# A transformer-like gate network on one core: the powers of the norms in two halves, and a new order of the steps in the middle batches

## The reference

```python
xn = layernorm(x)
s = attn(xn)                  # 16 heads of 16; rotary; the heads' logits are mixed (Wpre),
                              # softmax over all 512 keys, mixed again (Wpost), times v, Wout
g = silu(ffn(xn))             # 2 layers
x = x + s * g

# one layer of ffn: 8 heads of 64, windows of 128 tokens that see the window before
q, k, v = split(shift_token(x) @ wqkv)
q = l2norm(q) * q_scale;  k = l2norm(k) * k_scale      # t / max(norm(t), 1e-12)
q, k = rotary_xpos(q, k)
x = x + local_attention(q, k, v) @ wo
h = layernorm(shift_token(x)) * g + b
a, gate = split(h @ w1 + b1)
x = x + (a * gelu(gate)) @ w2 + b2
```

## Time and profile before

| | us |
|---|---|
| median of three runs | 5117.18 (5115.65 to 5125.04) |
| the profiled execution | 5116.08 |
| its span, first to last instruction | 5114.3 |
| busy: TensorE | 4966.4 |
| busy: VectorE | 3407.3 |
| busy: ScalarE | 3108.0 |
| busy: GpSimd | 2889.0 |

### The profile page before, as it was taken

The page is one execution under the profiler, slowest core; times in us unless marked ns, Lnnn a source line. Parts: engine busy times, 40 slices in busy tenths (PEclk is TensorE's granted clock), DMA queues, the critical chain, the costliest instruction groups (busy, mean ns, idle before and its releaser), DMA issues. The chain is left out here.

```text
span 5114.3 us, 184542 instructions
## 1 busy us (share of the span) xinstructions
PE 4966.4 (97%) x76184; PEld 4074.9 (80%) x76184; DVE 3407.3 (67%) x8316; ACT 3108.0 (61%) x8073; POOL 2889.0 (56%) x2509
## 2 busy tenths in 40 slices
PE   7999999999999999999999999999999999999998
PEld 5887888878878878787787877878888888878887
DVE  7667676666766667666676666766667676676765
ACT  4556665566655666556666566665566655666655
POOL 5546565565655656555565555655546555465654
PEclk9999999999999999999999999999999999999999
DMA  2321111121111211112111211211112112121111
GB/s 85 120 73 64 70 55 74 46 74 58 55 74 46 75 58 55 74 56 73 50 58 70 74 55 50 77 52 74 55 62 70 46 74 76 40 70 69 52 62 30
DMA packets 61263, 325.85 MB, mean 64 GB/s; under 512 B 6416, under 2 KB 23824, under 8 KB 43536
## 3 DMA queue, kind: packets, MB, share of 16 engines
q1 hardware_dynamic: 49632, 297.26, 15.4%
q0 software_dynamic: 10800, 16.78, 1.7%
HBM read 288.33 MB, written 34.08 MB: 63 GB/s over the span
## 5 line engine op out<-in xcount | busy, mean ns | idle before, releaser
L1603 POOL TENSOR_TENSOR q_lo<-q_mix,q_hi 128x512 fp32r<-128x512 f32 x512 | 661.0, 1291 | 868.5 <-ACT q_hi L1059 868.4
L1072 ACT ACTIVATE probs<-bank_S,neg_max 128x512 f32<-128x512 f32 x1024 | 699.2, 684 | 738.9 <-DVE neg_max L1333 645.3
L772 PE MATMUL bank_S<-k_hi,q_lo 128*128 128x512 f32 x2048 | 878.4, 429 | 38.9 <-POOL q_lo L1603 25.0
L1333 DVE TENSOR_REDUCE neg_max<-bank_S 128x1 f32<-128x512 f32 x1024 | 696.2, 687 | 301.4 <-PE bank_S L774 296.1
L773 PE MATMUL bank_S<-k_lo,q_hi 128*128 128x512 f32 x2048 | 805.0, 393 | 0.7 <-issue 0.7
L774 PE MATMUL bank_S<-k_hi,q_hi 128*128 128x512 f32 x2048 | 805.3, 393 | 0.0
L1598 POOL TENSOR_TENSOR q_mix<-q_rope,w_pre 128x256 f32<-128x256 f32 x1024 | 634.7, 647 | 43.8 <-POOL q_lo L1603 0.4
L789 PEld LDWEIGHTS bank_M<-mixer_n,probs 64*64 64x64 f32 x32768 | 529.8, 135 | 156.5 <-issue 138.0
L789 PE MATMUL bank_M<-mixer_n,probs 64*64 64x64 f32 x32768 | 597.0, 221 | 8.7 <-DVE o_locT_lo L1442 3.4
L1629 POOL TENSOR_TENSOR l_probs<-l_probs,l_inv 128x1024 f32<-128x1024 f32 (+1 forms) x256 | 430.6, 1690 | 270.5 <-DVE l_inv L1436 269.6
L1614 POOL TENSOR_TENSOR inv_norms<-norms_c,minus_half 128x16 f32<-128x16 f32 x128 | 417.1, 3258 | 259.9 <-DVE norms_c L1370 258.1
(11 more groups left out here) (160 smaller groups left out, 11374.9 us busy)
## 6 DMA issues: line engine op xcount, KB each, us to landing
w_qkv_hi<-split_qkv SPq DMA_DIRECT2D x30, 1536.0 KB, 9.6
w_qkv_lo<-split_qkv SPq DMA_DIRECT2D x30, 1536.0 KB, 6.3
w_hi<-split SPq DMA_DIRECT2D x30, 1408.0 KB, 6.1
w_lo<-split SPq DMA_DIRECT2D x30, 1408.0 KB, 6.0
w_hi<-split SPq DMA_DIRECT2D x30, 768.0 KB, 5.3
w_lo<-split SPq DMA_DIRECT2D x30, 768.0 KB, 7.2
w_o_hi<-split_o SPq DMA_DIRECT2D x30, 512.0 KB, 3.7
w_o_lo<-split_o SPq DMA_DIRECT2D x30, 512.0 KB, 4.6
```

Source lines behind the costliest of these rows:

```text
L772: mm(bank[k][:], q_lo[q], k_hi[:, s, :], start=(s == 0), stop=False)
L1072: fn(probs[:, n % PB, :], bank[k][:], ACT.Exp, bias=neg_max[:, n % 2:n % 2 + 1], accum_out=row_sum[:, n % 4:n % 4 + 1]).then_inc(emptied[k ...
L1333: v.tensor_reduce(neg_max[:, n % 2:n % 2 + 1], bank[k][:], AX.X, ALU.max, negate=True)\
L1603: g.tensor_tensor(q_lo[:, c % QB], q_mix[:], q_hi[:, c % QB].bitcast(F32), ALU.subtract)\
```

## The change

Two things. GpSimd's part of `qkv` computes k's eight powers alone and signals them with a semaphore of their own (k_inv_done). Its part of `join` waits for those and for the addition, multiplies k, and then computes q's eight powers; the wait for the last reader of the old q powers moves there with them. And ORDER, the list of a middle batch, is a new arrangement of the same 363 steps. FIRST_ORDER and LAST_ORDER are as they were.

```diff
@@ GpSimd, qkv and join
                 pool.wait_ge(clip_done, now.at(clip_done, w + 1))
                 if now.past(w):
                     pool.wait_ge(k_ready, now.at(k_ready, w))
-                if now.past(l):
-                    unit = ("local_scores", (l - 1) % LAYERS, QUADS * t + QUADS - 1)
-                    pool.wait_ge(emptied["F1"], now.fill(unit, "F1", ago=not l))
-                g.tensor_tensor(inv_norms[:, t, :], norms_c[:], minus_half[:], ALU.pow).then_inc(inv_norm_done, 1)
+                g.tensor_tensor(inv_norms[:, t, H:2 * H], norms_c[:, H:2 * H], minus_half[:, H:2 * H], ALU.pow).then_inc(k_inv_done, 1)
 
             def join(step, l, t):
                 w = TW * l + t
-                pool.wait_ge(inv_norm_done, now.at(inv_norm_done, w + 1))
+                pool.wait_ge(k_inv_done, now.at(k_inv_done, w + 1))
                 pool.wait_ge(rot_added, now.at(rot_added, w + 1))
                 k_tok = qk_tok[:, 1, :].rearrange("p (h d) -> p h d", h=H)
                 g.tensor_tensor(k_tok, k_tok, inv_norms[:, t, H:2 * H, None].to_broadcast([P, H, HD]), ALU.mult)\
                     .then_inc(k_ready, 1)
+                if now.past(l):
+                    unit = ("local_scores", (l - 1) % LAYERS, QUADS * t + QUADS - 1)
+                    pool.wait_ge(emptied["F1"], now.fill(unit, "F1", ago=not l))
+                g.tensor_tensor(inv_norms[:, t, 0:H], norms_c[:, 0:H], minus_half[:, 0:H], ALU.pow).then_inc(inv_norm_done, 1)
```

The stretches of ORDER that the prediction speaks of (the line before and after; the list in between is new as well):

```diff
@@ ORDER, the start
-expand.0 part.0 expand.1 qkv.0.0 join.0.0 part.1 scores.0 scores.1 qkv.0.1 scores.2 expand.2 bound q_turn.0.0 mixers.0
-join.0.1 part.2 k_turn.0.0 expand.3 qkv.0.2 q_turn.0.1 k_turn.0.1 scores.3 scores.4 part.3 mix.0 join.0.2 mixers.1
-expand.4 qkv.0.3 part.4 q_turn.0.2 mix.1 scores.5 join.0.3 mixers.2 k_turn.0.2 scores.6 scores.7 expand.5 mix.2
-sigmoid.0 part.5 expand.6 q_turn.0.3 k_turn.0.3 mixers.3 scores.8 part.6 local_scores.0.0 scores.9 mix.3
-local_scores.0.1 weigh.0.0 scores.10 expand.7 mixers.4 values.0 sigmoid.1 part.7 local_scores.0.2 scores.11 p_turn.0.0
-weigh.0.1 mix.4 weigh.0.2 mixers.5 scores.12 sigmoid.2 expand.8 local_values.0.0 part.8 p_turn.0.1 expand.9 scores.13
-silu mix.5 sigmoid.3 gated p_turn.0.2 local_values.0.1 mixers.6 part.9 local_scores.0.3 scores.14 scores.15
+expand.0 part.0 expand.1 qkv.0.0 part.1 join.0.0 expand.2 scores.0 scores.1 qkv.0.1 q_turn.0.0 bound join.0.1 mixers.0
+k_turn.0.0 part.2 qkv.0.2 expand.3 mix.0 scores.2 scores.3 q_turn.0.1 join.0.2 mixers.1 k_turn.0.1 part.3 expand.4
+qkv.0.3 part.4 q_turn.0.2 mix.1 scores.4 scores.5 join.0.3 k_turn.0.2 q_turn.0.3 mixers.2 sigmoid.0 expand.5 scores.6
+part.5 k_turn.0.3 scores.7 expand.6 local_scores.0.0 mix.2 mixers.3 scores.8 weigh.0.0 local_scores.0.1 part.6
+scores.9 mix.3 weigh.0.1 p_turn.0.0 scores.10 sigmoid.1 sigmoid.2 expand.7 values.0 local_values.0.0 part.7 mixers.4
+local_scores.0.2 p_turn.0.1 scores.11 expand.8 mix.4 scores.12 mixers.5 weigh.0.2 sigmoid.3 silu local_values.0.1
+gated part.8 scores.13 local_scores.0.3 expand.9 mix.5 mixers.6 p_turn.0.2 scores.14 scores.15 local_scores.0.4 part.9
@@ ORDER, end of layer 0
-out_proj.0.2 expand.13 local_values.0.6 p_turn.0.7 scores.22 local_values.0.7 mixers.10 scores.23 out_proj.0.3 mix.10
-half_turn.0 mixers.11 part.13 scores.24 expand.14 shift_turn.0 mix.11 scores.25 scores.26 mixers.12 values.2 part.14
...
-up.0.1 hide.0.0 hide.0.1 up.0.2 part.16 up.0.3 hide.0.2 hide.0.3 up.0.4 up.0.5 hide.0.5 hide.0.4 scores.30 expand.17
-mix.14 scores.31 scores.32 mixers.15 down.0.0 down.0.1 down.0.2 down.0.3 part.17 expand.18 part.18 mix.15 x_turn.1
-expand.19 scores.33 qkv.1.0 join.1.0 part.19 qkv.1.1 join.1.1 values.3 q_turn.1.0 k_turn.1.0 qkv.1.2 mixers.16
-q_turn.1.1 k_turn.1.1 scores.34 join.1.2 scores.35 expand.20 mix.16 part.20 qkv.1.3 k_turn.1.2 q_turn.1.2 mixers.17
+expand.12 part.12 expand.13 scores.22 local_values.0.7 scores.23 mix.10 mixers.11 out_proj.0.3 half_turn.0 mix.11
+part.13 shift_turn.0 scores.24 project.0 scores.25 h_scale.0 expand.14 values.2 mixers.12 scores.26 h_turn.0 part.14
...
+up.0.4 up.0.5 hide.0.5 hide.0.4 scores.28 mix.13 scores.29 scores.30 mixers.14 part.16 down.0.0 down.0.1 expand.17
+down.0.2 part.17 down.0.3 expand.18 mix.14 x_turn.1 scores.31 scores.32 mixers.15 part.18 qkv.1.0 mix.15 join.1.0
+qkv.1.1 expand.19 scores.33 q_turn.1.0 join.1.1 k_turn.1.0 qkv.1.2 part.19 mixers.16 values.3 join.1.2 expand.20
+k_turn.1.1 q_turn.1.1 qkv.1.3 mix.16 q_turn.1.2 scores.34 scores.35 join.1.3 mixers.17 k_turn.1.2 project.1 part.20
@@ ORDER, the end
-local_values.1.7 mixers.26 project.2 expand.29 out_proj.1.3 part.29 expand.30 scores.54 half_turn.1 scores.55 mix.26
-mixers.27 part.30 scores.56 expand.31 shift_turn.1 mix.27 scores.57 scores.58 mixers.28 h_scale.1 values.6 part.31
...
-hide.1.1 scores.63 mix.30 mixers.31 up.1.2 up.1.3 mix.31 scale hide.1.2 hide.1.3 up.1.4 values.7 x_turn.0 up.1.5
-project.3 hide.1.5 hide.1.4 talk_k talk_q down.1.0 down.1.1 down.1.2 talk_v down.1.3
+scores.54 local_values.1.7 part.30 scores.55 out_proj.1.3 mix.26 half_turn.1 expand.31 mixers.27 scores.56
+shift_turn.1 mix.27 scores.57 scores.58 values.6 mixers.28 part.31 h_scale.1 scores.59 mix.28 mixers.29 scores.60
...
+up.1.2 hide.1.1 up.1.3 x_turn.0 values.7 hide.1.2 hide.1.3 up.1.4 up.1.5 hide.1.5 talk_k project.3 hide.1.4 talk_q
+down.1.0 down.1.1 down.1.2 down.1.3 talk_v
```

More of the change, by code:

```diff
@@ L147 @@
-part.22 mix.19 local_scores.1.2 scores.42 weigh.1.1 weigh.1.2 local_values.1.0 values.4 mixers.20 expand.23
-local_scores.1.3 p_turn.1.1 scores.43 mix.20 scores.44 local_values.1.1 part.23 mixers.21 weigh.1.3 p_turn.1.2
-scores.45 local_scores.1.4 expand.24 mix.21 part.24 mixers.22 scores.46 expand.25 weigh.1.4 out_proj.1.0
-local_values.1.2 p_turn.1.3 part.25 scores.47 mix.22 mixers.23 local_scores.1.5 scores.48 scores.49 mix.23
-local_scores.1.6 weigh.1.5 p_turn.1.4 local_values.1.3 expand.26 mixers.24 values.5 part.26 expand.27 local_scores.1.7
@@ L152 @@
-scores.50 out_proj.1.1 weigh.1.6 mix.24 p_turn.1.5 weigh.1.7 local_values.1.4 scores.51 local_values.1.5 part.27
-p_turn.1.6 mixers.25 scores.52 expand.28 out_proj.1.2 local_values.1.6 p_turn.1.7 part.28 mix.25 scores.53
-local_values.1.7 mixers.26 project.2 expand.29 out_proj.1.3 part.29 expand.30 scores.54 half_turn.1 scores.55 mix.26
-mixers.27 part.30 scores.56 expand.31 shift_turn.1 mix.27 scores.57 scores.58 mixers.28 h_scale.1 values.6 part.31
-scores.59 mix.28 mixers.29 h_turn.1 scores.60 scores.61 mix.29 mixers.30 up.1.0 up.1.1 hide.1.0 scores.62 norm
@@ new lines @@
+p_turn.0.3 local_values.0.2 weigh.0.5 part.10 mixers.8 values.1 local_values.0.3 p_turn.0.4 local_scores.0.6 mix.8
+scores.19 weigh.0.6 out_proj.0.1 local_values.0.4 p_turn.0.5 mixers.9 expand.11 local_scores.0.7 weigh.0.7
+local_values.0.5 p_turn.0.6 part.11 scores.20 scores.21 mix.9 out_proj.0.2 mixers.10 local_values.0.6 p_turn.0.7 store
+expand.12 part.12 expand.13 scores.22 local_values.0.7 scores.23 mix.10 mixers.11 out_proj.0.3 half_turn.0 mix.11
+part.13 shift_turn.0 scores.24 project.0 scores.25 h_scale.0 expand.14 values.2 mixers.12 scores.26 h_turn.0 part.14
@@ new lines @@
+scores.36 k_turn.1.3 q_turn.1.3 scores.37 mix.17 expand.21 part.21 mixers.18 local_scores.1.0 scores.38 scores.39
+weigh.1.0 local_scores.1.1 mixers.19 mix.18 scores.40 local_scores.1.2 p_turn.1.0 scores.41 mix.19 expand.22 part.22
+expand.23 scores.42 mixers.20 weigh.1.1 weigh.1.2 local_scores.1.3 local_values.1.0 values.4 part.23 scores.43
+scores.44 mix.20 mixers.21 p_turn.1.1 local_scores.1.4 scores.45 expand.24 mix.21 weigh.1.3 scores.46 weigh.1.4
+local_values.1.1 part.24 expand.25 mixers.22 p_turn.1.2 scores.47 local_scores.1.5 mix.22 mixers.23 weigh.1.5
@@ new lines @@
+out_proj.1.0 scores.48 scores.49 part.25 expand.26 mix.23 p_turn.1.3 local_values.1.2 part.26 local_scores.1.6
+values.5 local_values.1.3 mixers.24 weigh.1.6 p_turn.1.4 scores.50 scores.51 expand.27 mix.24 part.27 expand.28
+local_scores.1.7 out_proj.1.1 mixers.25 weigh.1.7 project.2 local_values.1.4 part.28 p_turn.1.5 scores.52 expand.29
+local_values.1.5 p_turn.1.6 scores.53 mix.25 out_proj.1.2 part.29 mixers.26 local_values.1.6 p_turn.1.7 expand.30
+scores.54 local_values.1.7 part.30 scores.55 out_proj.1.3 mix.26 half_turn.1 expand.31 mixers.27 scores.56
@@ L159 @@
+shift_turn.1 mix.27 scores.57 scores.58 values.6 mixers.28 part.31 h_scale.1 scores.59 mix.28 mixers.29 scores.60
+scores.61 mix.29 mixers.30 h_turn.1 scores.62 scores.63 mixers.31 mix.30 norm up.1.0 hide.1.0 up.1.1 mix.31 scale
+up.1.2 hide.1.1 up.1.3 x_turn.0 values.7 hide.1.2 hide.1.3 up.1.4 up.1.5 hide.1.5 talk_k project.3 hide.1.4 talk_q
+down.1.0 down.1.1 down.1.2 down.1.3 talk_v
 """
@@ L493, in gate_network_kernel @@
         clip_done = sem("clip_done", WL)
+        k_inv_done = sem("k_inv_done", WL)
         inv_norm_done = sem("inv_norm_done", WL)
```

9 lines of the change are left out of this document (2 added, 7 removed).

## The result

The changed kernel takes 5146.14 us (median of 4 runs, 5140.49 to 5151.79), the kernel before 5116.41 beside it (5111.84 to 5125.04): ratio 1.0058, 95% interval 1.0046 to 1.0069. It is 0.6% slower. Forecast was 5096 in a range of 5070 to 5121. The profiled execution took 5140.49, the shortest of the four; its span is 5138.7. The granted clock over the span was 0.996 before; after, it was 0.994 in the runs of 5140.5 and 5141.7, and 0.993 in those of 5150.6 and 5151.8.

What follows compares the result with a forecast made beforehand. TensorE, busy 4966.4 of 5114.3 us, was taken to bound the kernel by work plus gaps. Each of 14 middle batches loses 4.8 and gains 3.5 us, 18 us in all; with 2.5 elsewhere, 5116.1 becomes 5096, range 5070 to 5121.

Steps and rivals of the forecast that it cites:

- all seven gaps that were to go: TensorE waits at scores.2, k_turn.1.1, k_turn.1.0, qkv.1.0, x_turn.0, k_turn.0.3, mix.5 go: 4.8 us per middle batch.
- scores.32's wait: TensorE's 0.9 us wait for ScalarE's probabilities stays and moves to scores.30.
- they cost nothing there: q's eight powers, now behind VectorE's addition, are needed over 15 us later, so cost nothing.
- the 0.39 us a window called hidden: Extra GpSimd work per window from splitting the powers, hidden under TensorE as long as q_lo comes in time.
- q_turn.0.3: Right behind k_turn.0.2, TensorE waits for VectorE's whole rotary addition: 1.45 us a batch, bounds 0 to 2.0.
- down.1.0: Tail step needing hidden_lo, expected some 1.8 us before it is asked for: no cost.
- VectorE's crowding: Sigmoid reciprocals no longer spread: waits at mix.4, mix.5, local_scores.0.0, together 1.05 us a batch, between 0.3 and 3.5.
- The second rival: Slower, 5130: VectorE's packed reciprocals reach mix.4 in full, 3.0 us more a batch; chance 0.15.
- mix.0: Comes 4 us earlier, with bound on ScalarE ahead of its mixers: 0.1 us a batch.
- half_turn.0: Right behind out_proj.0.3, whose result VectorE must first add into x_mid: 0.65 us a batch.
- shift_turn.1: Only one scores step stands between it and half_turn.1: 0.25 us a batch.
- The first rival: No change, 5106 to 5118: removed gaps come back at other steps; chance 0.22 together with the fourth rival.

Runs made afterwards that it cites:

- Experiment 8: Kernel before, powers unsplit, with two middle-batch moves: part.1 ahead of join.0.0, k_turn.1.1 behind scores.34. 5085.9 us, ratio 0.9941.
- experiment 12: Kernel before with part.1 ahead of join.0.0, k_turn.1.1 behind scores.34, powers split but both halves together ahead of k's multiplication. 5099.3 us, ratio 0.9971.
- experiment 2: Changed kernel's new order, but with the sixteen powers in one instruction. 5143.4 us, ratio 1.0060.
- experiment 7: Changed kernel with five steps moved (scores.5, hide.1.4, half_turn.0, scores.24, mixers.0) and the sixteen powers in one instruction. 5113.4 us, ratio 0.9986.
- Experiment 3: Changed kernel with part.4 (GpSimd's q_lo) moved behind q_turn.0.3. 5139.5 us, ratio 1.0042.
- Experiment 4: Changed kernel with hide.1.4 moved ahead of talk_k. 5135.1 us, ratio 1.0041.
- experiment 11: Changed kernel with sigmoid.2 moved behind mix.4, which put it beside sigmoid.3. 5168.7 us, ratio 1.0092.
- experiment 5: Changed kernel with scores.5 moved between k_turn.0.2 and q_turn.0.3. 5133.2 us, ratio 1.0035.
- experiment 6: Changed kernel, split kept, with five steps moved in the middle batches (scores.5, hide.1.4, half_turn.0, scores.24, mixers.0): the repaired order. 5112.8 us, ratio 0.9989.

## Why the prediction was wrong

**The bound and what goes: right.** TensorE's work stayed, its gaps decided, and all seven gaps that were to go went, 64 us of 67, at the named steps. The 0.18 us for each gap's broken overlap was a little high: the seven waits sum to 50 us and their slots to 64, 0.14 a gap, and the two largest (waits of 16.2 and 14.6, slots of 17.2 and 15.6) had 0.07 each. scores.32's wait moved to scores.30 unchanged. Experiment 8 adds that two of these gaps, alone, are worth 31 us.

**The powers: right in size, wrong in "they cost nothing there".** 1.64 us and the long form paid once, as forecast; k's waits fell to 1.4. But q's half holds norms_c, which the clip needs free: I looked for who needs the result and not for who needs the input released. In the new order this costs 1.9 us of VectorE's time, in the old one 11.3. And the 0.39 us a window called hidden is not: with both halves together three steps still wait for it (experiment 12). Whether the split costs depends on the order: 0.19% in the old one, 0.43 with the two moves, nothing in the new one, repaired or not, where what it wins at k_turn.0.0 comes back a few steps on (experiments 2 and 7).

**q_turn.0.3, priced at 1.45: the step that failed first.** "TensorE waits for a whole addition: 1.23 plus about 0.2 for two signals" took the addition alone. It was 2.1 to 2.6, +36.4 instead of +20.3, since GpSimd's q_lo held the addition at 1.8 to 2.3. Even the bound of 2.0 was too low. Experiment 3 gives 1.44 with part.4 out of the way. The rows had shown the conflict in its other direction (the powers' long form beside the same addition), and I priced it there alone.

**down.1.0, costed at nothing.** "I get hidden_lo some 1.8 us before down.1.0 asks for it" used hidden_lo at its undisturbed 1.3 us. The two take 4.02, 1.4 more, and the step waited 0.90, its slot growing by 1.2: +16.3. Experiment 4 takes it away.

**VectorE's crowding, 1.05 a batch: not there.** No wait at mix.4, mix.5 or local_scores.0.0. These 14.7 us were charged for nothing and hid part of the miss. The second rival, "slower", built on them: its direction came true, its reason did not. The mechanism is real, but had slack: one reciprocal of 1.74 more ahead of mix.5 made it wait 0.7, so about 1.0 was spare there (experiment 11). At local_scores.0.0 the move of one scores step used the slack up and made a wait of 0.9 (experiment 5). So such a term can't be priced from its neighbours alone; it depends on how late the whole queue runs.

**What I did not see: 24 us.** values.0 waits for bank M0, which ScalarE's copy empties (0.6), k_turn.0.1 for bank M1, which VectorE's copy empties, mix.11 has no waited-for engine in the trace. The waits at k_turn.0.1 and mix.0 are there only with the split (experiment 2). The small terms at half_turn.0 and shift_turn.1 were right to 1 us over the span; mix.0 cost 6.2 instead of 1.4.

**Half clock, costed at nothing: 8.6 us.** No term allowed for TensorE running slower behind a long wait. 6.5 us of it are among the other steps, whose sum of -4.8 hides them. It was read from kept traces afterwards; no run was made for it, but the stretches at scores.6 are gone where the wait is 1.5 or none (experiments 3, 5 and 6).

**The sum.** 16 us from the blocked addition, 16 from down.1.0, 24 from the unseen steps and 5 from mix.0 are 61 against the forecast, 15 from the missing crowding for it. That makes 46, less some 2 in the small terms and the other steps: from -18 to +26 in the middle batches of the profiled execution. The other 5 us up to the medians are not in any trace; the two longer runs had the lower clock. The first rival gave this way, "gaps come back at other steps", 22% and called 1.1 us more a batch enough for no change; it was 3.1. None of the rivals held the cause, "slower, 5130" came nearest in time by luck, and the range ended 25 us too low.

## What to carry to other kernels

Where a reorder puts a two-input VectorE operation on the path, list what GpSimd runs in that microsecond, and price the operation at its own time plus what GpSimd's instruction still has to run. Behind a new wait, read the granted clock in a window of a few microseconds, as neither the page's slices nor the busy share show it. Before splitting an instruction, ask which buffer its later half keeps from being overwritten, not only who waits for its result. And make order changes one step at a time with the ledger by step: two moves, one that let GpSimd write q_lo before it multiplies k and one that gave k_turn.1.1 cover that stood ready, won 31 us, while a full reorder took away 64 us of gaps and made 95 of others.

## What the hardware showed that was not expected

- A clip of 128x16 elements, 0.17 us, is held as fully as a long instruction: 1.19 us beside a q_lo of 1.30. A small operation is held as long as a large one.
- The price of `pow` lies on a straight line: 1.02 us for 4 columns, 1.64 for 8, 2.90 for 16. In two halves set back to back the second took 1.78 in the mean, though alone in its place 1.64.
- The hold of `pow` goes one way. In the kernel before, all 77 additions that start inside GpSimd's sixteen powers take 1.20 to 1.23 us (one of them is at 709.18 in batch 2, inside the powers from 706.69 to 709.59). All 47 powers that start inside an addition take 3.81 to 3.92 instead of 2.90. A q_lo holds the addition until it ends.
- Behind the wait of 2.1 to 2.6 us at q_turn.0.3 the granted clock was 0.50 for 3.4 us in five of fourteen batches, at about 1.5 us of time each; behind the wait of 1.5 us at the same step (experiment 3) in none, but behind 1.4 us at mix.11 once.
